# Four seams of a four-layer kernel rewritten: wide router products, weights rounded in the recurrence, shared weights split in the turn, a bisection with three candidates

## What is computed

```python
# L0: attention to 2 keys made of cond_1024, then a top-2 router over 8 experts, capacity 320
gates = jax.nn.softmax(x_flat @ router_w + router_b, axis=-1)
h = jax.nn.gelu(jnp.einsum('ecd,edh->ech', buf, w1) + b1[:, None, :], approximate=False)
# L1: top-2 of 4 experts per batch row plus a shared expert, then 8 dense experts
shared = jax.nn.gelu(context_c @ sw1 + sb1, approximate=True) @ sw2 + sb2
logits = (xt @ Wr + br) / TEMP
f_m = jnp.sum(jnp.maximum(Xs - tau_m, 0.0) ** inv_am1, axis=-1, keepdims=True) - 1.0   # 25 halvings
# L2: a recurrence over 64 steps, then each of 8 experts takes its 512 best tokens
next_h = jnp.tanh(xw_t + prev_h @ Wh)
G, idx = jax.lax.top_k(scores.T, k)
# L3: hyperbolic attention and FFN with a modulation, then a gated FFN in FP4
q = _GRID[idx] * jnp.sign(xn) * scale          # blocks of 16, of x, h and the three weights
gate = fp4_linear(x, w_gate)
y = fp4_linear(x, w_up)
h = jax.nn.silu(gate) * y
return fp4_linear(h, w_down)
```

## Time and profile before

| | us |
|---|---|
| median of the runs | 2452.9 (2451.99 to 2453.13) |
| the profiled execution, its span | 2452.52, 2450.8 |
| PE busy | 2078.2 (85%) |
| DVE busy | 1348.9 (55%) |
| ACT busy | 978.6 (40%) |
| POOL busy | 253.0 (10%) |
| recurrence, first tanh to last transpose | 1393.07 to 1489.77 |
| MoE of layer 0, the starts of L619 for experts 1 to 7 (counted from 0) | 133.20, 150.17, 170.63, 191.00, 211.38, 231.77, 252.15 |
| mean granted clock of TensorE | 0.90 of 2.4 GHz |

### The profile page before, as it was taken

The page is one execution under the profiler, slowest core; times in us unless marked ns, Lnnn a source line. Parts: engine busy times, 40 slices in busy tenths (PEclk is TensorE's granted clock), DMA queues, the critical chain, the costliest instruction groups (busy, mean ns, idle before and its releaser), DMA issues. The chain is left out here.

```text
span 2450.8 us, 34137 instructions
## 1 busy us (share of the span) xinstructions
PE 2078.2 (85%) x13331; PEld 1676.0 (68%) x13331; DVE 1348.9 (55%) x2555; ACT 978.6 (40%) x1938; POOL 253.0 (10%) x207
## 2 busy tenths in 40 slices
PE   6698789999799999999999886489956777885886
PEld 5388678888687888888888776378933554554554
DVE  2589555777576443444443213656546556454885
ACT  2143355555353444444444321035333354554222
POOL 1234200000000000000000002247720000000000
PEclk7699889999899999999999996689977867897989
DMA  2465322233112211111000000354363001000000
GB/s 78 164 191 143 64 69 69 70 103 103 36 35 73 49 35 35 35 52 35 26 9 1 10 4 2 127 173 118 69 141 102 2 19 35 18 18 36 1 9 26
DMA packets 111562, 146.02 MB, mean 60 GB/s; under 512 B 6744, under 2 KB 94727, under 8 KB 111144
## 3 DMA queue, kind: packets, MB, share of 16 engines
q1 hardware_dynamic: 101292, 130.00, 17.6%
q0 software_dynamic: 10112, 13.85, 3.3%
HBM read 121.85 MB, written 21.99 MB: 59 GB/s over the span
## 5 line engine op out<-in xcount | busy, mean ns | idle before, releaser
L1584 DVE TENSOR_TENSOR m_h_lo<-m_hf,m_h_hi 128x512 fp32r<-128x512 f32 x256 | 172.0, 689 | 358.6 <-ACT m_hf L1559 356.9
L1556 ACT ACTIVATE m_h_hi<-m_h_ps,m_bT 128x512 fp32r<-128x512 f32 x256 | 177.0, 691 | 367.3 <-PE m_h_ps L396 347.4
L1559 ACT ACTIVATE m_hf<-m_h_ps,m_bT 128x512 f32<-128x512 f32 x256 | 175.0, 684 | 0.0
L604 POOL DMA_INDIRECT token_sums<-e_y,slot_row x56 | 145.3, 2594 | 167.7 <-DVE e_y L712 155.6
L674 ACT ACTIVATE e_h_hi<-e_h_ps,e_b1T 128x320 fp32r<-128x320 f32 (+1 forms) x128 | 77.9, 609 | 176.3 <-PE e_h_ps L396 171.1
L1296 DVE TENSOR_TENSOR c_h_lo<-c_hf,c_h_hi 128x512 fp32r<-128x512 f32 x120 | 82.2, 687 | 74.2 <-ACT c_hf L1255 73.1
L736 DVE TENSOR_TENSOR e_h_lo<-e_hf,e_h_hi 128x320 fp32r<-128x320 f32 (+1 forms) x128 | 74.1, 588 | 85.6 <-ACT e_hf L677 84.1
L1823 POOL MEMSET n_bias<- 128x256 f32 x1 | 0.3, 312 | 1081.9 <-POOLq L59 1081.9
L1252 ACT ACTIVATE c_h_hi<-c_h_ps,c_b 128x512 fp32r<-128x512 f32 x88 | 61.7, 701 | 109.7 <-PE c_h_ps L396 109.1
L396 PE MATMUL m_y_ps<-m_h_hi,l_w_1hi 128*128 128x512 f32 x256 | 100.3, 392 | 3.4 <-issue 3.4
L396 PE MATMUL m_y_ps<-m_h_hi,l_w_0hi 128*128 128x512 f32 x256 | 99.7, 389 | 1.4 <-ACT m_gT L1570 1.4
(11 more groups left out here) (646 smaller groups left out, 5565.6 us busy)
## 6 DMA issues: line engine op xcount, KB each, us to landing
cT<-in_L_ffn_W_dram SPq DMA_DIRECT2D x30, 1024.0 KB, 5.5
res<-in_L_cond_ew_dram SPq DMA_DIRECT2D x22, 1024.0 KB, 5.5
cT<-in_L_ffn_w_dram SPq DMA_DIRECT2D x16, 1024.0 KB, 6.0
res<-gates_rows SPq DMA_DIRECT2D x8, 1024.0 KB, 15.3
l_mod<-modulation_rows SPq DMA_DIRECT2D x16, 512.0 KB, 6.8
token_rows<-d_tok SPq DMA_DIRECT2D x2, 2112.0 KB, 9.3
token_sums<-res SPq DMA_DIRECT2D x2, 2048.0 KB, 8.3
res<-token_sums SPq DMA_DIRECT2D x8, 512.0 KB, 5.5
```

Of the source, the lines that this page charges most:

```text
L604: pool.indirect_dma_start(out=sums, out_offset=bass.IndirectOffsetOnAxis(ap=st.slot_row[0:r, e, j:j + 1], axis=0), in_=y[0:r, e % 2, j, :] ...
L1556: act.activation(hs[0][:, f, :], h_ps[:, f % HB, :], ACT.Relu, bias=bT[:, at:at + 1])
L1559: act.activation(hf[:, f % HB, :], h_ps[:, f % HB, :], ACT.Relu, bias=bT[:, at:at + 1]).then_inc(act_done, 1)
L1584: dve.tensor_tensor(hs[1][:, f, :], hf[:, f % HB, :], hs[0][:, f, :].bitcast(F32), ALU.subtract).then_inc(h_ready, 1)
```

## The change

1. All three routers: the router's weights, padded from 8 to 32 columns with zeros that POOL writes, are now what is loaded into the array, and 512 tokens are the moving data: 2 halves x 4 groups = 8 matmuls of 512 columns, each group of tokens in its own 32 columns of the array and its own 32 partitions of one bank. ACT copies the bank, PE transposes it in four pieces, DVE adds the bias in four small operations. The products wait for the weights only. In the L1 dense FFN the four transposes stand inside the first unit of the first layer. The wait for the modulation's store moves from the L0 router to dispatch.
2. QuantWeights moves from layer 0's MoE to the recurrence: from step 4 on, after each step's transpose, DVE does one or two of its operations (five parts a piece), PE one transpose of rounded weights after the next step's inputs (from step 20; six remain after the last step), ACT one copy of a bank per group; SP stores them turned. The L3 FFN loads them as they are used.
3. The shared expert's weights of layer 1 are loaded into cT2 behind the last expert of MoE0 and split in the t1 block. The rows' way back is asked for there too, behind eight small loads; PE turns both halves of a block before the next. The condition starts with unit 0's first layer; the gate's small matmuls, the selection and the lists come after it, one unit later. The dense FFN's small loads come at the condition's end. In layer 3 the rows' way back is asked for after the first modulation load instead of at MoE2's end.
4. Bisection with 3 candidates instead of 4: candidate 0 is left out, and the level so far is kept beside the others.

The core of the diff:

```diff
+            sp.dma_start(self.bias[:, :], b.partition_broadcast(P)).then_inc(self.bias_in, 16)
+        sp.wait_ge(self.w_zero, 1)
+        sp.dma_start(self.w[:, :, 0:E8], W.rearrange("(c p) e -> p c e", p=P)).then_inc(self.w_in, 16)
...
-    def make_logits(self, pe, st, srcT):
-        pe.wait_ge(self.w_in, 16 * self.inputs)
-        for t in range(NT):
-            out = self.ps[:, t * E8:(t + 1) * E8]
-            for k in range(KC):
-                last = pe.matmul(out, srcT[:, k, t * P:(t + 1) * P], self.w[:, k, :], start=(k == 0), stop=(k == KC - 1))
+    def make_products(self, pe, srcT):
+
+        pe.wait_ge(self.w_in, 16)
+        for k in range(KC):
+            for g in range(NB):
+                last = pe.matmul(self.products_ps[g * GC:(g + 1) * GC, :], self.w[:, k, :], srcT[:, k, g * BLK:(g + 1) * BLK],
+                                 start=(k == 0), stop=(k == KC - 1), skip_group_check=True)
+        last.then_inc(self.products_made, 1)
+
+    def keep_products(self, act):
+        act.wait_ge(self.products_made, 1)
+        act.activation(self.logitsT[:, :], self.products_ps[:, :], ACT.Copy).then_inc(self.products_kept, 1)
+
+    def turn_products(self, pe, st):
+        pe.wait_ge(self.products_kept, 1)
+        for j in range(TPB):
+            last = pe.transpose(self.ps[:, j * P:(j + 1) * P], self.logitsT[:, j * P:(j + 1) * P], st.ident[:, :])
...
-    WAYS = 4
+    WAYS = 3
-                pool.memset(bits[:, w:w + 1], w << (BITS - 2)).then_inc(c1, 1)
+                pool.memset(bits[:, w:w + 1], (w + 1) << (BITS - 2)).then_inc(c1, 1)
...
+                ada.wait_stored(sp)
...
-                if e == 1 and rounding:
-                    rounding.load(sp)
-            if rounding:
-                rounding.store(sp)
-            sp.wait_ge(y_out, 16 * E8 * J)
-            for b in range(NB):
-                sp.dma_start(st.res[:, b * TPB:(b + 1) * TPB, :],
-                             sums[b * BLK:(b + 1) * BLK, :].rearrange("(t p) d -> p t d", p=P)).then_inc(res_in[b], 16)
+            if shared:
+                shared.load(sp, w1_split, w2_split)
...
-                    if e >= 1:
-                        next(pieces, None)
...
+            small.load(sp, st)
+            back.load(sp, st)
+            dve.wait_ge(w1_hi, 1)
+            dve.tensor_tensor(w1[1][:, :, :], shared.w1_raw, w1[0][:, :, :].bitcast(F32), ALU.subtract).then_inc(split, 1)
+            dve.wait_ge(w2_hi, 1)
+            dve.tensor_tensor(w2[1][:, :, :], shared.w2_raw, w2[0][:, :, :].bitcast(F32), ALU.subtract).then_inc(split, 1)
+            for g, (b, c) in enumerate(groups):
+                if g % 2 == 0:
+                    dve.wait_ge(turned, g + 1)
...
+            act.wait_ge(shared.w1_in, 16)
+            act.activation(w1[0][:, :, :], shared.w1_raw, ACT.Copy).then_inc(w1_hi, 1)
+            act.wait_ge(shared.w2_in, 16)
+            act.activation(w2[0][:, :, :], shared.w2_raw, ACT.Copy).then_inc(w2_hi, 1)
...
+            up(0)
...
-            pe.wait_ge(b_kept, 1)
-            up(0)
+            down(0)
             pe.wait_ge(selected, 1)
             pe.matmul(ps[:, 0, 0:E4], st.ones[0:B, :], chosen[:, :], start=True, stop=True, skip_group_check=True)
             pe.matmul(ps[0:B, 0, E4:2 * E4], st.tri[0:B, 0:B], chosen[:, :], start=False, stop=True,
                       skip_group_check=True).then_inc(counted, 1)
-            down(0)
+            up(1)
...
-            up(1)
             pe.wait_ge(columns_set, 1)
             down(1)
...
+            next_small.load(sp, st)
...
+                    if n == 0:
+                        turn_logits()
+
+            def turn_logits():
+                pe.wait_ge(products_kept, 1)
+                for j in range(TPB):
+                    last = pe.transpose(l_ps[:, j * P:(j + 1) * P], logitsT[:, j * P:(j + 1) * P], st.ident[:, :])
+                last.then_inc(logits_made, 1)
...
-            pe.wait_ge(r_in, 32)
-            for t in range(NT):
-                for k in range(KC):
...
+            pe.wait_ge(wr_in, 16)
+            for k in range(KC):
+                for g in range(NB):
+                    last = pe.matmul(lT_ps[g * GC:(g + 1) * GC, :], wr[:, k, :], srcT[:, k, blk(g)], start=(k == 0),
+                                     stop=(k == KC - 1), skip_group_check=True)
+            last.then_inc(products_made, 1)
...
+            turn_steps = rounding.turn_steps(pe, st)
             for s in range(S):
                 if s >= 1:
                     pe.wait_ge(kept, s)
                 recur(s)
                 if s + 1 < S:
                     inputs(s + 1)
+                if s >= rounding.FIRST_STEP:
+                    next(turn_steps, None)
+            for _ in turn_steps:
+                pass
 
...
+            pieces = rounding.pieces(dve)
             for s in range(S):
                 dve.wait_ge(tanhed, s + 1)
                 dve.transpose(dst[:, :, :, s], h[:, s % 2, :].rearrange("p (j c) -> p j c", c=C)).then_inc(kept, 1)
+                if s >= rounding.FIRST_STEP:
+                    next(pieces, None)
+            for _ in pieces:
+                pass
             dve.wait_ge(kept, S)
...
-            sp.dma_start(gu[:, :, :].rearrange("p j k -> p (j k)"), kept_gu).then_inc(gu_in, 16)
-            sp.dma_start(dn[:, :, :].rearrange("p c i -> p (c i)"), kept_dn).then_inc(dn_in, 16)
+            sp.dma_start(guT[:, :, :].rearrange("p c n -> p (c n)"), kept_gu).then_inc(gu_in, 16)
+            sp.dma_start(dT[:, :, :].rearrange("p j d -> p (j d)"), kept_dn).then_inc(dn_in, 16)
...
-            turn_weights()
             turn_in(0)
-            pe.wait_ge(w_kept, len(groups))
+            pe.wait_ge(gu_in, 16)
+            pe.wait_ge(dn_in, 16)
```

More of the change, by code:

```diff
@@ L401, with dispatch_phase @@
 PADS = BLK
-def dispatch_phase(nc, sem, st, tag, srcT, rows, sums):
+def dispatch_phase(nc, sem, st, tag, srcT, rows, sums, ada=None):
     NS = PADS // P
@@ L753, in _ @@
             scale(E8 - 1)
-            for _ in pieces:
-                pass
+    return y_out, 16 * E8 * J
 class State:
@@ L1394, in _ @@
             dve.wait_ge(columns_set, 1)
-            for u in range(1, UNITS):
+            x_low(2)
+            for u in range(2, UNITS):
                 for f in range(FC):
@@ L1819, in _ @@
             sp.dma_start(bias[0:1, :], b.unsqueeze(0)).then_inc(bias_in, 16)
+            rounding.load(sp)
+            rounding.store(sp)
         @block.gpsimd
@@ L3050, in _, with l1_phases @@
                 add(p)
-def l1_phases(nc, sem, st, a):
+def l1_phases(nc, sem, st, a, back, shared):
     with ExitStack() as mem:
```

485 lines of the change are left out of this document (310 added, 175 removed).

## The result

The changed kernel takes 2418.8 us (median of 4 runs, 2412.7 to 2422.6), the kernel before 2452.4 (4 runs, 2446.8 to 2453.1): a ratio of 0.9862, interval 0.9843 to 0.9881. It is faster by 1.4%, but that is 33.6 us and not the 54.7 forecast, and the time lies above the range of 2388 to 2414. The profiled execution, 2422.6 us with a span of 2420.8, is the slowest of the four; its parts are read against the 2450.8 of before.

A forecast was written before the change was run, and what follows sets the result against it. PE, working 2078.2 of 2450.8 us, was taken as the bound; savings of 9.4 + 22.1 + 4.5 + 11.7 + 2.5 + 4.5 = 54.7 us from the profiled 2452.5 gave 2398 us, range 2388 to 2414.

The forecast's parts named there:

- the sentences on the recurrence: Recurrence loop: rounding pairs fit, barely, into DVE's idle 1.3 us a step; PE's transposes add 1.5 us (0 to 8).
- Rival (b): Recurrence: transposes cost their whole 0.27 us (7.6), pairs delay DVE's transpose by 0.3 (3.6); 2408 us, 16%.
- Rival (d): Recurrence: DVE's rounding pairs lie in the chain itself, adding 67 us; slower than before at 2461 us, 2%.
- Loads at the condition's start move: 0.3: Layer 3's condition: moving loads at its start saves 0.3 us.
- rows are asked for some 3.5 us later, at worst: Layer 1's start: returning rows requested at most some 3.5 us later, within a part saving 4.5 us (2 to 7).
- Rival (e): Layer 1's shared-weights seam: eight loads ahead of the rows cost more than the early layer gives; 2403 us, 7%.
- the L3 FFN: Layer 3's FFN: removing 34 transposes saves 6.3 us, less 2.1 for PE starting at half clock.
- MoE0's 22.1: Layer 0's MoE: moving the rounding out makes PE the next bound and saves 22.1 us (18 to 24).
- rival (a): Routers: the four column groups run one after another, products take 13.8 us; 2418 us, 10%.
- The L2 router's 6.65: L2 router: faster logits save about 2.9 us until POOL's selects bind; one cache-reduce less in bisection saves 3.75.
- Rival (c): L2 router: softmax beside POOL's selects blocks DVE and holds bisection back 3 to 6 us; about 2402 us, 8%.
- the L0 router, 9.4: L0 router: faster products and an earlier modulation save 9.4 us, between 2 (serial) and 14 (modulation at full clock).

The follow-up runs named there:

- e10: Changed kernel with the recurrence's state and input columns packed for PE's weight loads, using ACT copies, all values kept: 2382.5 us, ratio 0.9725.
- e2: Changed kernel with all rounding, PE transposes and their copies moved behind the recurrence's last step: 2452.6 us (one run).
- e7: Changed kernel with the recurrence's matmuls loading the packed condition as weights in all steps, recurrence values left out: 2385.9 us (one run).
- e11: Changed kernel with only the recurrence's state packed, input columns still loaded at a stride: 2394.6 us (one run).
- e3: Changed kernel with PE's transposes and ACT's copies moved behind the recurrence's last step, rounding left inside: 2419.8 us (one run).
- e4: Changed kernel with layer 1's returning rows asked for ahead of the eight small loads: 2412.3 us, ratio 0.9834.

## Why the prediction was wrong, point by point

**The step that failed most** is in the sentences on the recurrence: that pairs of rounding operations, "0.52 to 1.05 us each (twice the 526 ns of the earlier trace rows at most)", fit into DVE's 1.3 us of idle time. The 526 ns were measured in MoE0, beside PE loads of packed weights, and I carried them to a place where PE loads weights at a stride of 256 bytes. There a long two-input operation has 1.2 us on average and up to 1.4; the pair of L1942 and L1943 has 1.5 to 1.9 us, the other pairs 1.0 to 1.7, and the steps took 1.76 us on average instead of 1.52. The term of 1.5 us for the loop was 15.3. That the pairs fit was right only for operations at their lone length: in e10 they do, at a cost of 3.5 us. This mechanism is shown: by e2 (alone the operations are normal), e7 and e10 (with packed columns they are normal inside the loop), and e11 (only those beside strided loads are long). What it is in the strided loads that does it is not shown. Rival (b) had the place, a late hand-over by DVE, but priced it at 0.3 us in 12 steps; its other half, 7.6 us for PE's transposes, is refuted by e3. Rival (d) named the mechanism that would have made the kernel slower; it would have needed 0.9 us a step, and 0.24 came.

The trace of before could have shown it. Two rows of its loop, weight loads of 32 columns by the same engine, the first packed and the second strided:

```profile
L1831 PEld LDWEIGHTS n_sums<-n_bias,n_ones 128*32 128x32 f32 x496 | 17.6, 134 | 0.0
L1835 PEld LDWEIGHTS n_sums<-n_wx,cT 128*32 128x32 f32 x1008 | 38.4, 234 | 0.0
```

134 against 234 ns for the same shape says that the stride is paid for (the bias's weights are ones that lie packed); that the engines beside pay too, only an experiment could say.

**The second** is "Loads at the condition's start move: 0.3" in layer 3. I credited the loads that moved and did not price the one that was now late: the rows, which 8 statistics operations and all that follows wait for. It cost 4.4 us on average and 9.7 in the profile. The rule to price the wait behind a moved DMA was applied in layer 1 and not here.

**The third**, "rows are asked for some 3.5 us later, at worst": they were 6.3 later, since the block's own start after the last scatter (5.2 us) came on top, where before they were asked for inside the MoE's block. Of the 7.55 us by which the first layer was to be earlier 4.7 came; what follows in the condition is 4.3 longer, where I had counted 3.1 for the gate's matmuls and the wait for columns. Rival (e) named this: it priced the seam at 5 us less, and 4.1 less came. By e4 3.0 us of it is the order of two calls.

**The fourth**, the L3 FFN: the first product came 5.5 us earlier in its stage, where 6.3 was costed, and lost 2.8 at half clock (I had taken 2.1) and 2.2 more further on, which no run explains. 0.5 is left of 4.2.

**Right:** MoE0's 22.1 (22.8), with its period of 17.0. The products' overlap: 3.64 us for eight, against 3.45 forecast and 13.8 for rival (a), which falls. The Trainium skill ("TensorE: Matmul & The Clock Gate", Part 3) measured a speedup of 2.38 for three packed column groups, and the estimate from it was 4.3 us; the trace lies nearer to full overlap. The L1 dense router's 11.7 (12.9). The L2 router's 6.65 (6.9), with the first count right behind POOL's last select; the faster logits gain only until POOL is the later one, 3.2 us. Rival (c) did not appear there at its size: beside the selects one DVE operation of the softmax, with two inputs, has 0.46 us instead of 0.29, and the others keep their time. Too low was the L0 router, 9.4 for 14.6, since the clock rose during the modulation; that this was possible stood in its bound of 14, and that it came to pass was luck for the total. Without it the miss would have been larger: the errors of the four steps add up to 32 us, and 7 came back here and in parts 1 and 2. It is chance as well that rival (a)'s 2418 is the measured time: its mechanism did not occur.

## What to carry to other kernels

Before work is put beside other work, compare each duration with its own value in that place or in a place with the same neighbours: the price of an operation belongs to what runs beside it. Where PE loads weights at a large stride inside a loop, try an idle engine's copy to a packed buffer; here two copies of 0.31 us a step on ACT took 0.39 us off each step of the kernel before, and made room for 45 us of other work at a cost of 3.5. And for each DMA that a change moves, look for the engine that waits for it on the other side, even if the change is elsewhere.
